# Cross attention and a mixture of experts: each token through all eight experts, or through its two chosen ones

## The reference

```python
x = x + xattn(layernorm(x), ctx, ctx, W_Q, b_Q, W_K, b_K, W_V, b_V, W_O, b_O)   # 2 x 512 tokens, 16 heads
x = x + ffn(layernorm(x), ...)
# ffn, for each token of 256 values:
shared = (silu(xf @ sw1) * (xf @ sw3)) @ sw2                  # 512 hidden values
s = sigmoid(xf @ router_w.T)
_, topk_idx = top_k(s + router_bias, 2)                       # 2 of 8 experts
gates = s_sel / (s_sel.sum() + 1e-9)                          # comb has them, zero for the six others
h = gelu(einsum('nd,edh->neh', xf, ew1))                      # all eight experts, 256 hidden values
y = einsum('neh,ehd->ned', h, ew2)
routed = einsum('ned,ne->nd', y, comb)
```

## Time and profile before

| | us |
|---|---|
| median of three runs | 373.49 |
| the runs | 373.35, 373.49, 1775.43 |
| time of the profiled execution | 377.48 |
| its span, from the first instruction to the last | 375.7 |
| TensorE busy | 358.6 |
| VectorE, ScalarE, GpSimd busy | 275.9, 223.8, 133.9 |

### The profile page before, as it was taken

One profiled execution on the slowest core, in us unless ns is written; L12 is line 12 of the kernel. 1 busy time (PEld: TensorE's weight loads), 2 busy tenths in 40 slices (PEclk: granted clock), 3 DMA queues, 4 the chain that ended last, 5 costly groups with the idle time before them and its releaser, 6 DMA issues.

```text
span 375.7 us, 7081 instructions
## 1 busy us (share of the span) xinstructions
PE 358.6 (95%) x2704; PEld 223.4 (59%) x2704; DVE 275.9 (73%) x424; ACT 223.8 (60%) x405; POOL 133.9 (36%) x176
## 2 busy tenths in 40 slices
PE   5878998999999999999999999999999999999996
PEld 2665565333333333333643454489899998989985
DVE  5767988799999999999589418075577865755455
ACT  5553446698899899989578977622243341524422
POOL 5032475013053353425244243000277664026700
PEclk9998999799999999999999999999999999999999
DMA  7679990015060615234100200020032332003301
GB/s 274 258 253 337 305 352 6 2 64 170 9 226 5 202 32 145 90 93 142 56 9 1 63 4 2 2 58 2 0 110 86 87 86 84 0 2 112 114 1 56
DMA packets 21610, 36.62 MB, mean 97 GB/s; under 512 B 5684, under 2 KB 14516, under 8 KB 19892
## 3 DMA queue, kind: packets, MB, share of 16 engines
q1 hardware_dynamic: 21576, 36.17, 29.6%
HBM read 27.15 MB, written 7.34 MB: 92 GB/s over the span
## 4 chain that ended last, share of the span: by engine, by line
PE 85%; DVE 5%; ACT 3%; DMA 3%; SPq 1%; issue 1%; ACTq 0%
PE psum L1073 42%; PE psum L1209 18%; PE psum L1136 14%; PE psum L1143 8%; DVE negm L968 3%; DMA PB<-in_ctxT_dram 2%; ACT PB L733 1%; SPq L463 1%; PE psum L1222 1%; DMA qs_d<-SWH 1%; ACT TMP L777 1%; DMA QS<-qs_d 1%; DVE XT L863 1%; PE psum L1192 1%; DVE R L855 1%
## 5 line engine op out<-in xcount | busy, mean ns | idle before, releaser
L968 DVE TENSOR_REDUCE negm<-psum 128x1 f32<-128x1024 f32 x128 | 154.1, 1222 | 15.9 <-PE psum L1143 15.3
L733 ACT ACTIVATE PB<-psum 128x512 f32<-128x512 f32 x256 | 138.4, 598 | 29.1 <-PE psum L1136 20.5
L1143 PE MATMUL psum<-KS,QS 64*128 64x512 f32 x256 | 87.5, 463 | 5.8 <-DMA QS<-qs_d 2.8
L1136 PE MATMUL psum<-QS,KS 64*128 64x512 f32 x256 | 92.1, 458 | 0.4 <-ACT PB L733 0.3
L1209 PE MATMUL psum<-PB,VA 128*17 128x256 f32 x1024 | 81.0, 390 | 2.1 <-ACT TMP L777 2.1
L748 ACT ACTIVATE PB<-psum 128x512 f32<-128x512 f32 x40 | 23.9, 600 | 81.4 <-PE psum L1073 81.4
L1136 PEld LDWEIGHTS psum<-QS,KS 64*128 64x128 f32 x256 | 38.3, 187 | 50.0 <-ACT PB L733 40.0
L640 POOL TENSOR_SCALAR R<-RAW 128x512 fp32r<-128x512 f32 x32 | 20.6, 644 | 99.7 <-PE psum L1073 73.4
L1073 PE MATMUL psum<-XT,R 128*128 128x512 f32 x192 | 46.7, 392 | 0.0
L1209 PEld LDWEIGHTS psum<-PB,VA 128*17 128x17 f32 x1024 | 17.4, 95 | 46.4 <-issue 35.4
L1143 PEld LDWEIGHTS psum<-KS,QS 64*128 64x128 f32 x256 | 35.4, 189 | 12.2 <-DVE negm L968 5.0
(11 more groups left out here) (139 smaller groups left out, 365.5 us busy)
## 6 DMA issues: line engine op xcount, KB each, us to landing
RAW<-in_ew_dram SPq DMA_DIRECT2D x32, 256.0 KB, 2.7
KS<-ks_d SPq DMA_DIRECT2D x24, 256.0 KB
QS<-qs_d SPq DMA_DIRECT2D x48, 128.0 KB
ks_d<-SWH SPq DMA_DIRECT2D x8, 512.0 KB, 4.2
qs_d<-SWH SPq DMA_DIRECT2D x4, 512.0 KB, 4.4
RAW<-in_sw_dram SPq DMA_DIRECT2D x6, 256.0 KB, 2.8
x_sb<-in_x_dram SPq DMA_DIRECT2D x2, 512.0 KB, 5.2
PB<-in_ctxT_dram SPq DMA_DIRECT2D x2, 512.0 KB, 6.0
```

The source lines that it names most:

```text
L733: act.activation(PB[:, n % PR, i * N:(i + 1) * N], bank[t % 3], ACT.Exp, scale=DK ** -0.5).then_inc(exp_done, 1)
L968: dve.tensor_reduce(negm[:, g % 2, r // QT, r % QT:r % QT + 1], psum[:, k0:k0 + 2, :].rearrange("p a n -> p (a n)"), AX.X, ALU.max, negate ...
L1136: pe.matmul(bank[t % 3], KS[s][rows, j, kp * P:(kp + 1) * P], QS[s][rows, j, :], start=True, stop=True).then_inc(scores_done, 1)
L1143: return pe.matmul(ring_bank(("max", m), half), QS[s][rows, j, qt * P:(qt + 1) * P], KS[s][rows, j, :], start=True, stop=True)
```

## The change

For each batch of 512 tokens there are 1024 pairs (token, expert). They are sorted by expert into 15 tiles of 128 places (NTL). `rank` counts on PE, by matmuls with triangular and full matrices of ones, how many earlier tokens chose each expert. `place` (49 instructions on DVE) turns that into a tile and a place for each pair and builds one-hot matrices. `table` multiplies them on PE, which gives each place its token, and PE then reads 15 numbers into registers, the offset of each tile's expert in the weights. `index` (10 instructions on DVE) makes the row numbers. The normalised tokens are stored to memory by SP, and POOL gathers 128 rows for a tile by an indirect DMA. A tile then has four stages: `tx` (two transposes), `th` (6 matmuls of 256 columns, tokens stationary, weights streamed from the address in a register), `tt` (two transposes), `ty` (6 matmuls). ACT and DVE take the results of `tx` and `tt` as a high and a low part, ACT applies Gelu after `th` and copies after `ty`, and POOL scatters the 128 rows back to memory by another indirect DMA. Each stage has one PSUM bank. `combine` loads the two rows of each token and adds them with their gates. All 15 tiles are computed whatever the inputs are, with a place without a pair filled by row 0. The 16 weight chunks of the experts are now loaded and split once and kept for both batches; before they were loaded for each.

```diff
-HR = 12
+NTL = 15
+XR = 8
+TR = 4
...
             todo += [("router", 0)]
+        if r == 26:
+            todo += [("rank", 0), ("place", 0)]
         return todo
...
+    pairs = [(tb, k) for tb in range(2) for k in range(HT)]
     steps += [("h_part", i // 4, i % 4 // KT, i % KT) for i in range(8, 16)]
-    steps += [("h", 0), ("h", 1), ("oproj_part", 1), ("h", 2), ("h", 3)]
...
+    steps += [("h", 0), ("h", 1), ("h", 2), ("h", 3), ("table", 0), ("index", 0), ("oproj_part", 1)]
+    steps += [("sums", NG - 1), ("norm", NG - 1), ("y", 0, 0), ("y", 0, 1), ("oproj", 1), ("y", 0, 2), ("y", 0, 3)]
...
+    def tile_steps(b, i):
+        return [(kind, NTL * b + i - d) for d, kind in enumerate(("tx", "th", "tt", "ty")) if 0 <= i - d < NTL]
+    for i in range(NTL + 3):
+        steps += tile_steps(0, i)
+        if i == 0:
+            steps += [("stats2", 1, t) for t in range(4)] + [("var2", 1)]
+        if i == 2:
...
+        if i == 3:
             steps += [("xpose2", 1)]
...
+        if i == 5:
+            steps += [("logits", 1, t) for t in range(4)]
+        if i == 6:
+            steps += [("router", 1)]
+        if i == 9:
+            steps += [("rank", 1)]
+        if i == 10:
+            steps += [("place", 1)]
+        if i == 16:
+            steps += [("table", 1), ("index", 1)]
+    steps += [("h", p) for p in range(4, 8)]
+    for i in range(NTL + 3):
+        steps += tile_steps(1, i)
+        if i == 4:
+            steps += [("combine", 0)]
+        if i >= NTL - 1:
+            steps += [("y", 1, i - NTL + 1)]
+    steps += [("combine", 1)]
...
-        if st[0] in ("max", "oproj", "xpose2", "y") or st == ("negmax", 0):
+        if st[0] in ("max", "oproj", "xpose2", "rank", "table") or st == ("negmax", 0):
             ring_at[st] = len(ring_at)
...
+        if st[0] == "y" and st[2] == 3:
+            ring_at[("y", st[1])] = len(ring_at)
...
-                for c in range(2 * g, min(2 * g + 2, EARLY)):
+                for c in range(2 * g, 2 * g + 2):
                     load_chunk(c)
+            for c in range(2 * NG, EARLY + 4):
+                load_chunk(c)
             sums_out(NG - 1)
             sums_in(NG - 1)
-            for c in range(EARLY, NCH):
+            for c in range(EARLY + 4, NCH):
                 load_chunk(c)
+            store_xn(1)
...
+            for b in range(B):
+                for i in range(TR):
+                    sp.wait_ge(ys_stored[i], ys_count(i, b))
+                if b:
+                    sp.wait_ge(combined, 2)
+                src = ys_d[b][0:SPARE, :].rearrange("(k p t) d -> p k (t d)", k=2, t=4)
+                for i in range(2):
+                    sp.dma_start(yk[:, 2 * i:2 * i + 2, :], src[:, :, i * N:(i + 1) * N]).then_inc(yk_loaded[i], 16)
+                for i in range(2):
+                    sp.wait_ge(combined, 2 * b + i + 1)
+                    t = 4 * b + 2 * i
+                    sp.dma_start(ot[:, b, 2 * i:2 * i + 2, :], x_sb[:, t:t + 2, :]).then_inc(stored, 16)
+            sp.wait_ge(stored, 64)
...
-                        pool.wait_ge(ring_full, ring_at[("y", q // NE * (NE + 1) + 1 + q % NE)] + 1)
+                    if c == EARLY:
+                        pool.wait_ge(scores_done, tiles_upto(UG * (NG - 1) - 1))
+                    if c == EARLY + 4:
+                        pool.wait_ge(scores_done, ALL_TILES)
                 pool.tensor_scalar(hi, RAW[:, c % 2, :], 1.0, 1.0, ALU.mult, ALU.mult).then_inc(pool_chain, 1)
...
+            def gather(n):
+                b, i = n // NTL, n % NTL
+                if i == 0:
+                    pool.wait_ge(index_ready, b + 1)
+                    pool.wait_ge(xn_stored[b], 16)
+                    pool.wait_ge(pv_done, 4 * HG * KP)
+                if n >= XR:
+                    pool.wait_ge(x_turned, n - XR + 1)
+                pool.indirect_dma_start(xg[n % XR], None, xn_d[b], bass.IndirectOffsetOnAxis(gidx[:, b, i:i + 1], 0))\
+                    .then_inc(xg_loaded[n % XR], 16)
+            def scatter(n):
+                b, i = n // NTL, n % NTL
+                pool.wait_ge(y_out, n + 1)
+                pool.indirect_dma_start(ys_d[b], bass.IndirectOffsetOnAxis(sidx[:, b, i:i + 1], 0), ys[n % TR], None)\
+                    .then_inc(ys_stored[n % TR], 16)
             for c in range(EARLY, NCH):
-                if c == EARLY + 4:
+                split_chunk(c)
+            for b in range(B):
+                for i in range(5):
+                    gather(NTL * b + i)
+                if b == 0:
                     guess_rstd(4, slice(4, 8))
-                split_chunk(c)
+                for i in range(NTL):
+                    if i + 5 < NTL:
+                        gather(NTL * b + i + 5)
+                    scatter(NTL * b + i)
...
+            def tile(kind, n):
+                if kind == "tx":
+                    act.wait_ge(x_turned, n + 1)
+                    if n >= TR:
+                        act.wait_ge(h_done, n - TR + 1)
+                    elif n == 0:
+                        act.wait_ge(ring_full, ring_at[("oproj", 1)] + 1)
+                    act.activation(pbt[n % TR][:, 0, 0], turned(0), ACT.Copy).then_inc(x_hi, 1)
+                elif kind == "th":
+                    act.wait_ge(h_done, n + 1)
+                    if n >= TR:
+                        act.wait_ge(h_turned, n - TR + 1)
+                    act.activation(hs[n % TR], bank[1][:, 0:D], ACT.Gelu).then_inc(gelu_done, 1)
+                elif kind == "tt":
+                    act.wait_ge(h_turned, n + 1)
+                    if n >= TR:
+                        act.wait_ge(y_done, n - TR + 1)
+                    act.activation(pbt[n % TR][:, 1, 0], turned(2), ACT.Copy).then_inc(h_hi, 1)
+                else:
+                    act.wait_ge(y_done, n + 1)
+                    if n >= TR:
+                        act.wait_ge(ys_stored[n % TR], 16 * (n // TR))
+                    act.activation(ys[n % TR], bank[3][:, 0:D], ACT.Copy).then_inc(y_out, 1)
             act.wait_ge(exp_zero, 1)
...
+            def place(b):
...
+                oh = [rt[b][:, 6 + k] for k in range(2)]
+                if b == 0:
+                    dve.wait_ge(order_consts, 13)
+                    dve.wait_ge(pv_done, 4 * HG * KP)
...
+                ring_wait(("rank", b))
+                dve.tensor_copy(rk, ring_bank(("rank", b))[:, 0:40]).then_inc(slot_empty(("rank", b)), 1)
...
+                link(dve.tensor_tensor(cube(328, 4, NE), over.rearrange("p (t e) -> p t e", e=NE), mid1(first, 4), ALU.add))
+                for k in range(2):
+                    ks = slice(4 * k, 4 * k + 4)
+                    dve.tensor_tensor(cube(360, 4, NE), oh[k], inside.rearrange("p (t e) -> p t e", e=NE), ALU.mult)
+                    dve.tensor_tensor(cube(392, 4, NE), oh[k], cube(328, 4, NE), ALU.mult)
+                    link(dve.tensor_tensor(cube(424, 4, NE), oh[k], comb[:, 4 * b:4 * b + 4, :], ALU.mult))
+                    dve.tensor_reduce(pos[:, ks], cube(360, 4, NE), AX.X, ALU.add)
+                    dve.tensor_reduce(col[:, ks], cube(392, 4, NE), AX.X, ALU.add)
+                    link(dve.tensor_reduce(gk[:, b, k], cube(424, 4, NE), AX.X, ALU.add))
+                for i in range(8):
+                    dve.tensor_scalar(onehot[b][:, i, :], column[:, :], pos[:, i:i + 1], None, ALU.is_equal)
+                    dve.tensor_scalar(token[b][:, i, 0:NTL], column[:, 0:NTL], col[:, i:i + 1], lane[:, :],
+                                      ALU.is_equal, ALU.mult)
+                    last = dve.tensor_scalar(token[b][:, i, NTL:], column[:, 0:NTL], col[:, i:i + 1], float(i + 1),
+                                             ALU.is_equal, ALU.mult)
+                last.then_inc(place_ready, 1)
...
+            def index(b):
...
+                ring_wait(("table", b))
+                row, which, late, at, none = (w[:, NTL * i:NTL * (i + 1)] for i in range(5))
+                dve.tensor_copy(w[:, 0:2 * NTL], ring_bank(("table", b))[:, 0:2 * NTL])\
+                   .then_inc(slot_empty(("table", b)), 1)
...
+                link(dve.tensor_scalar(at, at, -1.0, 0.0, ALU.add, ALU.max))
+                dve.tensor_copy(gidx[:, b, :], at)
+                link(dve.scalar_tensor_tensor(out=late, in0=late, scalar=float(S), in1=at, op0=ALU.mult, op1=ALU.add))
+                link(dve.tensor_tensor(none, none, spare[:, :], ALU.mult))
+                dve.tensor_tensor(sidx[:, b, :], late, none, ALU.add).then_inc(index_ready, 1)
+            def combine(b):
+                for i in range(2):
+                    dve.wait_ge(yk_loaded[i], 16 * (b + 1))
+                    for k in range(2):
+                        for t in range(2):
+                            dst = x_sb[:, 4 * b + 2 * i + t, :]
+                            last = dve.scalar_tensor_tensor(out=dst, in0=yk[:, 2 * i + k, t * D:(t + 1) * D],
```

(70 more changed lines are left out.)

306 lines of the change are left out of this document (181 added, 125 removed).

## The result

The changed kernel takes 432.83 us (median of four runs, 428.39 to 433.68) against 374.07 for the kernel before on the same chip. The ratio of the two kernels leaves out the runs in which the chip was in a slower state, and keeps for the changed kernel 428.39 and a fifth run of 422.77. It is 1.138, with a 95% interval of 1.120 to 1.157, so the time to set beside 374 is some 425.6 us. On a second chip, beside three of the experiments, the changed kernel took 426.5, a ratio of 1.130 (1.118 to 1.142). So 409 was in the right direction, and the range of 390 to 440 holds both numbers. But 409 was 24 us under the median, 17 under the 425.6 and 17.5 under the 426.5. The runs also spread more than those of before: the granted clock of one run differs from that of another (0.922 in the run of 422.77, 0.904 in the profiled one of 428.39, 0.892 in one of 432.64).

A forecast was written before the change was run, and what follows sets the result against it. PE was taken as the bound, saving 31 us by estimate. Stages to 273.4, then 61.5, 11, 45.4 and 14 reach 405.3; 3 arithmetic and 2.5 clock bring the span to 411, own time 413, median 409; range 390 to 440.

The forecast's parts named there:

- The prediction's own case: Whole kernel: PE's saving is lost to waits, median 409 us, 392 to 425 from its small terms; chance 0.61.
- the rivals of POOL and of the registers: Tiles: indirect DMAs at 2.6 us, or register arithmetic at 0.19 each in PE's way; 434 either way; chances 0.12, 0.08.
- the terms for arithmetic and clock: Tiles: 3 us for register arithmetic on PE's sequencer, 2.5 for a lower clock after PE's stops.
- Before the tiles: Stretch up to the first tile: PE 12 us later, first tile at 273.4.
- The two waits: Before the tiles: first h_part waits 4.6 us for DVE's slot; oproj_part waits for the table copy, until 260.2.
- Its rule for DMA descriptors: POOL can't write DMA descriptors during DVE's 2-port operations; gathers held through place(1) would make the time 411.
- The rival: Clock decides: PE at half level for a third of the tiles, +20 us, 429; chance 0.06.
- Batch 0's tiles: 15 tiles in 18 steps: 35.3 us at 1.96 plus DVE's blocks, logits and register reading, 61.5, to 334.9.
- The shared expert: Between the batches' tiles: 4 x 2.74 = 11 us on PE, covering five gathers, to 345.9.
- Batch 1's tiles: 45.4 us: 35.3 for 18 steps plus shared outputs, combine(0) and POOL's loop holding seven steps at 2.6; to 391.3.
- POOL decides: Batch 1 and first gathers: indirect DMA costs 2.6, the pair 5.2 a step, about 25 longer, 434; chance 0.12.
- The tail: After the last ty: copy, scatter, two loads, combining and store take 14 us, to 405.3.

The follow-up runs named there:

- e3: The changed kernel with POOL splitting chunks 14 to 17 only after place(0) is done: 428.88 us, ratio 1.130 to the kernel before.
- e4: The changed kernel with 92 useless matmuls of 512 columns filling four of PE's waits: 423.0 us, ratio 1.120 to the kernel before.
- e7: The changed kernel with route(1) and place(1) spread three instructions at a time, and batch 1's register loads in four portions: 413.03 us, ratio 1.100.
- e1: The changed kernel with gathers issued 7 tiles ahead of the scatters instead of 5: 427.86 us, ratio 1.135 to the kernel before.
- e6: The changed kernel without batch 1's gathers, so its tiles compute on stale rows: 419.56 us, ratio 1.115 to the kernel before.
- e12: e11 with batch 1's gathers split, eight before its first tile and seven behind first steps, add_y(0) moved, 10 useless matmuls near 260: 390.06 us, 1.034.
- e2: The changed kernel with constant expert addresses (wrong weights), no register arithmetic and no loading of 15 registers: 421.42 us, ratio 1.114.
- e11: The changed kernel with e7's edits, reordered work before the first tile, 15 gather buffers, batch 1's shared outputs after the last tile, small edits: 399.8 us, 1.067.

## Why the prediction was right, and where its sizes were off

The direction was right for the reason given: what the matmuls save is paid back by waits at the places named, with the releasers named. The number is another matter. The prediction's own case ran from 392 to 425, and the measured 425.6 to 432.83 lies at its upper end and above; the range up to 440 was there for the rivals of POOL and of the registers at 434, and neither has that price. So the range holds the result in part by luck. By its own steps, on the clock of the profiled spans (411 foreseen, 426.2 measured), the stages miss by some 21 us together, and 5.5 of these are the terms for arithmetic and clock, which the prediction had beside the stages:

- **Before the tiles**: 273.4 foreseen, 283.1 measured, the largest miss (+9.7). The two waits are at the places named and have the releasers named. Two things were mis-sized. One is DVE's work, taken from rows in a stretch in which POOL was nearly idle, while the change moves POOL's splits beside it: the first `h_part` stands 2.8 us later than foreseen, 2.6 of them this contention by e3, and the shared expert's reads take 2.4 us more. The slow index(0) costs nothing here, since the first tile at 283.11 waits for no gather. The other is half clock: from the first `h_part` to the end of the attention product it is 19.1 us at a mean clock of 0.77, for 16.2 foreseen, and from `oproj_part` to the first tile 14.6 for 13.2, together 4.3. The prediction's own sentence on the 1.06 us row told of this exclusion; it asked only what it would do to the gathers, not what POOL's new work would do to DVE. The Trainium skill (SBUF — State Buffer, SBUF: two separate sides) says that a GpSimd instruction and certain kinds of DVE instructions take a shared port pair, whichever starts first for its whole instruction, while the other is blocked; the trace agrees (230.46 + 0.94 ends with POOL's instruction). Its rule for DMA descriptors was not seen in POOL's time: the gathers at 325.14 and 327.85, in the middle of place(1), took 0.98 and 0.97 us like all others.
- **The clock**: 2.5 foreseen as a term; some 8 us came back in the filled stretches of e4's profiled execution, which is one execution. The rival was ruled out too far by the 0.96 of the first 40 us, where PE's gaps are short and many. Behind the stops shown above that end at 236.3, 312.4, 333.1 and 347.9 PE runs at half clock; the row at 347.88 shows it, 1.64 us for six matmuls that take 0.96 in a step of 1.87.
- **Batch 0's tiles**: 61.5 foreseen, 66.2 measured. PE's waits beside route(1) and place(1) are 6.2 and 7.4 (6.5 and 9.7 foreseen; place took 9.2, not 11.0); the miss goes with steps at half clock, and with the waits filled e4 gets 4.4 us back here. e7 shows what these blocks cost together with the register loads of batch 1: 11 us.
- **The shared expert**: 11.7 for 11.
- **Batch 1's tiles**: 45.4 foreseen, 51.8 measured. An indirect DMA costs POOL 0.98 us and 0.30 of gap, 1.28 for the estimated 1.2. But the step was worked out as half of a loop, 2.6, and measured at 3.1, and e1 and e6 show that the loop was not the bound: POOL's two DMAs for each tile are 2.56 by themselves. What lies over 2.56 was not taken apart; half clock behind the waits is a part of it. That 2.6 is near 2.56 is chance; the mechanism was the rival's ("POOL decides"), at half its price for a DMA and a quarter of its 25 us (e6: 5.8).
- **The tail**: 13.3 for 14.
- **Registers**: 3 us for arithmetic and 1.7 for table and load foreseen; the rows show nothing for the first, and 3.9 from the start of `table` to the next `ty` for the second.

Last, the median: the foreseen one was placed 4 us under the profiled execution, as in the kernel before; here the median of four lies 4.4 us over the profiled execution.

Open: why the end or the signal of some of PE's products comes late (the "remote" stops). They come with indirect DMAs, the longest is where a row of gathers meets the 1 MB load, and they shrank when the row was broken up (4.6 to 2.8), but e12 changed two other things as well, and no run took the load away from beside such a row. Open too is how much of the growth is half clock in all: no run fills every wait.

## What to carry to other kernels

Work that is saved on the engine that bounds a kernel is worth its time only while nothing new stands in that engine's way. Here 31 us of matmuls went by the estimate, and the waits for the order of the pairs, for POOL's DMAs and for the tail cost more than that. The order of the pairs of batch 1 is made on DVE in two long blocks; with these cut into pieces of three instructions behind each tile, and the register loads spread, the kernel was 11 us faster. When a change moves work of POOL beside a chain of small DVE instructions, price the chain with one instruction of POOL for each that it meets. And count the time of all that an engine issues for each step (here two DMAs of 1.28 us against a step of 1.87) before working out latencies.

## What was not expected of the hardware

- DVE instructions of 0.16 to 0.19 us took 0.9 to 1.1 beside POOL's elementwise ones of 1.26; a reduction of 0.19 did not.
- 15 registers read by PE stop it for 3.5 us; spread between products they show no stop (e7), and the address arithmetic between the matmuls of a tile shows none either (e2).
- An indirect DMA of 128 rows of 1 KB takes POOL 0.98 us, with 0.30 between two.
- Beside indirect DMAs the semaphore of a PE product came up to 5.7 us after the product's modelled end, in e11 once 6.7, and kept ACT idle for up to 7.8 us; in the kernel before there is no such case.
